# A one-core attention and FFN kernel: the hand-written orders of four engines are laid out anew

## Chip, cores and metric

The kernel runs on one core of a Trainium2 chip. The metric is the device time of one execution in microseconds (us), lower is better. The core has a matrix engine (TensorE, PE here, with its weight loads as PEld), VectorE (DVE), ScalarE (ACT), GpSimd (POOL) and a queue engine (SP) that issues transfers.

## What is computed

The reference, cut to what matters. The inputs x and ctx have shape (8, 128, 256): 8 batches, 128 channels that are 16 heads of 8, and 256 positions.

```
def xattn(k, v, q, taps, D):            # k = v = ctx, q = layernorm(x), 16 heads of 8
    kv = einsum('bhil,bhjl->bijhl', k, v)
    y = causal convolution of kv with taps[h] along l (length 256)
    out = y + kv * D[h]
    return einsum('bijhl,bhil->bjhl', out, q)
x = x + xattn(ctx, ctx, layernorm(x), taps, D)
h = layernorm(x)
x = x + (silu(h @ Wg.T) * (h @ Wu.T)) @ Wd.T     # W = (wq - 128) * s, 256 -> 704 -> 256
```

## The kernel before

The work runs in two stages that overlap. The first is the attention. For each of 16 heads `n` the products k_i k_j are made for 36 pairs of channels (`all_products` on DVE for heads 0 and 1; for the others `squares` on ACT and `pairs` on POOL). PE multiplies them with the head's Toeplitz matrix, which carries the taps and the skip D, in three float32 matmuls of 288 columns (`convolve_across`, `convolve_within`, together `convolve`; L985, L994, L996), two passes each. For heads 0 to 7 the matrix is loaded from memory, and DVE adds D to its diagonal (`direct`, L664). `multiply_terms(n)` on DVE (L731, L734, L738) multiplies the result, in PSUM, with q, in SBUF, and writes eight slots of terms. Two heads make a tile `t` of 128 rows of x, eight tiles in all.

q of a tile comes from a layernorm in small steps over three engines: `stats_of_q`, `moments_of_q`, `variance_of_q` on DVE, the power -1/2 `root_q` on POOL (L371), `shift_of_q` on DVE, `norm_q` on ACT (L488), a transposition by PE (`turn_q`, L939) and `evict_q` on ACT (L501, L504). The eight slots of a tile are summed by PE through transposing matmuls that accumulate in PSUM (`sum_terms`, L965). To spare PE, tiles 2 to 7 are merged beforehand: `merge_front` on POOL (L279), `merge_back` on DVE or, for tiles 5 to 7, on POOL (L287), and for tiles 3 to 7 `merge_last` on DVE (L296), which needs both others. ACT copies the wrapped channels first (`wrap`, L513), on which `merge_back` waits. Each merge reads two operands of 128x512 in SBUF and writes SBUF. `add_sum` on DVE adds the sum to x.

The second stage is the FFN, in four blocks `i` of two tiles. The same layernorm steps with the suffix f (`root_f`, L376), `turn_f` on PE (L947), then `high_f` on ACT and `low_f` on DVE (L717), which split the transposed rows in a high and a low float16 part. `gates(i, t)` on PE (L1018) gives gate and up for 128 hidden units (six chunks, the last one of 64), `gate` on ACT takes the silu, `hidden_units` on DVE (L746) the product, `hidden_high` on ACT and `low` on POOL or DVE (L257) split it in two parts. `downs` and `downs_last` on PE (L1037) multiply them with the third weight matrix, `scale_out` on DVE (L762) scales, `add` on POOL (L301) or `add_ffn` on DVE adds to x, and `store` sends the rows out. The convolutions use three PSUM tensors of two banks each (`conv`), which the gates share later; all transpositions of f, and of q from tile 6 on, and all sums share one bank (`turn`), so each must wait until its last reader is done.

Each engine executes its own list in order, and semaphores hold an instruction until what it needs is done. The lists are written out by hand, one call per line, at the end of each engine's function (POOL from L398, ACT from L545, DVE from L764, PE from L1060). Nothing else sets the order: a call that waits holds every call behind it on its engine. The waits stand in the helpers, for instance:

```
def sum_terms(t, free, count):
    ...
        wait(pe, all_merged, t + 1 - TWICE_MERGED)
    wait(pe, wrapped, t + 1)
...
def merge_last(eng, t):
    ...
    wait(eng, merged, t + 1 - UNMERGED)
    wait(eng, pool_back_merged if back_on_pool(t) else back_merged, back_count(t))
```

Of the kernel before, what the change touches and what calls it, by code (L numbers as in the profile page):

```python
# [74 lines left out]
def build(nc, x, ctx_skip, taps, matrices, wg_t, s_gate, wu_t, s_up, wd_t, s_down, taps_pad, out):  # L75
    with ExitStack() as ctx:
# [80 lines left out]
        q_ready = sem("q_ready")  # L157
# [210 lines left out]
        def _(pool):  # L368
# [77 lines left out]
            merge_front(nc.gpsimd, 5)  # L446
            pairs(15, 0, 2)
            merge_back(nc.gpsimd, 5)
            root_f(4)
            merge_front(nc.gpsimd, 6)  # L450
            low(0, 3)
            low(0, 4)
            merge_back(nc.gpsimd, 6)
            root_f(5)
            low(1, 0)
            low(1, 1)
            merge_front(nc.gpsimd, 7)
            low(1, 2)
            merge_back(nc.gpsimd, 7)
            root_f(6)  # L460
            add(0, 0)
            low(1, 3)
            low(1, 4)
            low(2, 0)
            root_f(7)
            low(2, 1)
            low(2, 2)
            add(0, 1)
            add(1, 0)
            add(1, 1)  # L470
            low(2, 3)
# [3 lines left out]
            low(3, 3)  # L475
            add(2, 0)
# [3 lines left out]
        def _(act):  # L480
# [75 lines left out]
            wrap(0)  # L556
            evict_q(1)
            act.wait_ge(k_loaded[3], 16)
            squares(4)
            norm_q(2)  # L560
            squares(5)
            squares(6)
            wrap(1)
            evict_q(2)
            squares(7)
            act.wait_ge(k_loaded[4], 16)
            squares(8)
            convert_gate()
            norm_q(3)
            wrap(2)  # L570
            squares(9)
            evict_q(3)
            norm_f(0)
            norm_q(4)
            convert_up()
            squares(10)
            high_f(0)
            evict_q(4)
            norm_f(1)
            squares(11)  # L580
            wrap(3)
            high_f(1)
            norm_q(5)
            convert_down()
            evict_q(5)
            act.wait_ge(scales_loaded, 3 * 16)
            gate(0, 0)
            wrap(4)
            gate(0, 1)
            hidden_high(0, 0)  # L590
            norm_q(6)
# [622 lines left out]
```

## Time and profile before

| | us |
|---|---|
| median of 3 runs | 76.41 |
| lowest, highest | 76.26, 76.46 |
| span of the profiled execution, first to last instruction | 74.5 |
| PE, DVE, POOL, ACT busy in it | 69.8, 61.7, 58.8, 45.5 |

No time of its own is given for the profiled execution beside its span; the median of the runs lies 1.9 us above that span. The profile gives for each engine its busy time, and for each instruction its start, its duration and what it waited for. Matmuls are pipelined: PE's rows overlap each other, and from one matmul to the next only the distance of their starts counts. The granted share of PE's clock was 0.997 over the span.

### The profile page before, as it was taken

The numbers are of one execution on the slowest core, as the hardware profiler recorded it, in microseconds if no ns is written. First come the engines' busy times: TensorE is split into PE (matmuls) and PEld (weight loads), VectorE is DVE, ScalarE is ACT, GpSimd is POOL, SyncE is SP. The second block draws the span as 40 slices with busy tenths as digits, with TensorE's granted clock in tenths as the row PEclk, the third lists the DMA queues.
The fourth block names the chain that finished last, engine by engine and source line by source line (L and its number), as shares of the span: only waits on it lengthen the run. The fifth ranks groups of instructions, "written<-read, shape, count | busy, mean of one in ns | idle before, by whom it ended". The sixth has DMA issues, their size and how long they took to land.

```text
span 74.5 us, 1494 instructions
## 1 busy us (share of the span) xinstructions
PE 69.8 (94%) x470; PEld 57.7 (77%) x470; DVE 61.7 (83%) x187; ACT 45.5 (61%) x115; POOL 58.8 (79%) x76
## 2 busy tenths in 40 slices
PE   5999989999999989999999999999999999999920
PEld 4666557988878848889798889797999989899810
DVE  0078899999988999999999899999968884586760
ACT  1503436464867879967746894657768796776400
POOL 6033587997999999899999999479998999339230
PEclk9999999999999999999999999999999999999998
DMA  0898999999997000000000000000002006000404
GB/s 8 235 254 230 372 315 364 324 382 392 361 356 224 29 0 0 0 0 4 9 0 0 0 0 4 0 0 0 0 13 70 0 0 210 1 9 0 140 1 141
DMA packets 7128, 8.29 MB, mean 111 GB/s; under 512 B 816, under 2 KB 6224, under 8 KB 7120
## 3 DMA queue, kind: packets, MB, share of 16 engines
q1 hardware_dynamic: 6768, 7.88, 33.0%
q10 hardware_dynamic: 352, 0.31, 1.2%
q8 instruction: 4, 0.07, 0.4%
q14 instruction: 4, 0.03, 0.2%
HBM read 7.12 MB, written 1.07 MB: 110 GB/s over the span
## 4 chain that ended last, share of the span: by engine, by line
PE 68%; POOL 16%; DVE 9%; issue 2%; ACT 1%; POOLq 0%; DVEq 0%
PE conv L1018 26%; PE down L1037 13%; POOL products L387 10%; PE conv L985 6%; PE turn L1058 5%; PE conv L994 5%; PE conv L996 5%; POOL rstd_q L371 4%; PE turn L965 3%; DVE terms L731 3%; PE turn L947 2%; PE turn L1037 2%; POOL terms L279 2%; DVE terms L734 1%; DVE terms L738 1%
## 5 line engine op out<-in xcount | busy, mean ns | idle before, releaser
L1018 PE MATMUL conv<-f_parts,wgu 128*128 128x256 f16 x176 | 22.1, 273 | 0.0
L387 POOL TENSOR_TENSOR products<-k_skip 128x512 f32<-128x512 f32 (+1 forms) x16 | 18.2, 1147 | 1.2 <-DMA k_skip<-ctx_skip 1.2
L1018 PEld LDWEIGHTS conv<-f_parts,wgu 128*128 128x128 f16 x176 | 16.6, 98 | 2.7 <-DVE hidden L746 0.2
L257 POOL TENSOR_TENSOR h_lo<-hidden,h_hi 128x256 fp32r<-128x256 f32 x18 | 13.1, 745 | 2.6 <-ACT h_hi L527 2.5
L746 DVE SCALAR_TENSOR_TENSOR hidden<-conv,su_sb,gate_act 128x256 f32<-128x256 f32 (+1 forms) x24 | 11.5, 482 | 3.0 <-ACT gate_act L522 2.8
L522 ACT ACTIVATE gate_act<-conv,sg_sb 128x256 f32<-128x256 f32 (+1 forms) x24 | 11.2, 467 | 4.2 <-PE conv L1018 3.9
L985 PE MATMUL conv<-products,toeplitz 128*128 128x288 f32 x32 | 11.3, 437 | 0.1
L731 DVE TENSOR_TENSOR terms<-conv,q_ext 128x512 f32<-128x512 f32 x16 | 10.9, 682 | 0.5 <-ACT q_ext L504 0.3
L994 PE MATMUL conv<-products,toeplitz 128*128 128x288 f32 x32 | 10.6, 413 | 0.3 <-DVE toeplitz L664 0.3
L996 PE MATMUL conv<-products,toeplitz 128*128 128x288 f32 x32 | 10.4, 406 | 0.0
L527 ACT ACTIVATE h_hi<-hidden 128x256 fp32r<-128x256 f32 x20 | 8.3, 413 | 3.4 <-DVE hidden L746 3.1
L1037 PE MATMUL down<-wd,h_hi 128*128 128x256 f32 x35 | 9.8, 307 | 0.0
L1037 PE MATMUL down<-wd,h_lo 128*128 128x256 f32 x35 | 8.8, 280 | 0.0
L734 DVE TENSOR_TENSOR terms<-conv,q_ext 128x384 f32<-128x384 f32 x16 | 8.8, 549 | 0.0
L488 ACT ACTIVATE q_rows<-x_sb,shift_q,rstd_q 128x256 f32<-128x256 f32 x8 | 4.8, 595 | 6.2 <-DVE shift_q L689 6.2
L279 POOL TENSOR_TENSOR terms<-terms 128x512 f32<-128x512 f32 x6 | 8.4, 1396 | 0.0
L965 PE MATMUL turn<-ident,terms 128*128 128x128 f32 x60 | 7.9, 273 | 0.0
L994 PEld LDWEIGHTS conv<-products,toeplitz 128*128 128x128 f32 x32 | 6.1, 197 | 2.3 <-issue 1.0
L965 PEld LDWEIGHTS turn<-ident,terms 128*128 128x128 f32 x60 | 7.0, 141 | 0.9
L996 PEld LDWEIGHTS conv<-products,toeplitz 128*128 128x128 f32 x32 | 6.1, 190 | 1.7
L371 POOL TENSOR_TENSOR rstd_q<-variance_q,minus_half 128x1 f32<-128x1 f32 x8 | 5.3, 664 | 2.6 <-DVE variance_q L684 2.6
L1037 PEld LDWEIGHTS down<-wd,h_hi 128*128 128x128 f32 x35 | 6.6, 189 | 0.5 <-DVE h_lo L257 0.2
(64 smaller groups left out, 121.6 us busy)
## 6 DMA issues: line engine op xcount, KB each, us to landing
k_skip<-ctx_skip SPq DMA_DIRECT2D x3, 384.0 KB, 5.9
toeplitz<-taps_pad SPq DMA_DIRECT2D x2, 512.0 KB, 8.6
out<-x_sb SPq DMA_DIRECT2D x7, 128.0 KB, 1.7
toeplitz<-matrices SPq DMA_DIRECT2D x3, 256.0 KB, 5.4
wg_int<-wg_t SPq DMA_DIRECT2D x1, 704.0 KB, 7.6
wu_int<-wu_t SPq DMA_DIRECT2D x1, 704.0 KB, 8.8
wd_int<-wd_t SPq DMA_DIRECT2D x1, 640.0 KB, 10.0
x_sb<-x SPq DMA_DIRECT2D x1, 512.0 KB, 5.1
```

Source lines behind the costliest of these rows:

```text
L257: eng.tensor_tensor(low_of(i, t), hidden[up_lanes(t), i % 2, t, :], high_of(i, t), ALU.subtract).then_inc(done, 1)
L279: eng.tensor_tensor(even, even, odd, ALU.add).then_inc(merged, 1)
L387: nc.gpsimd.tensor_tensor(view(products[:, n:n + 1], first * MADE + GROUP, [[MADE, halves], [GROUP, 4], [1, GROUP]]), view(k, 0, [[EXT * B ...
L522: nc.scalar.activation(gate_act[up_lanes(t), i % 2, t, :], gate_of(i, t), ACT.Silu, scale=sg_sb[gate_lanes(t), t:t + 1]).then_inc(gate_act ...
L731: dve.tensor_tensor(view(z, h, [[TERMS, HALVES], [P, 4], [to, GROUP]]), view(y, HALF0, [[COLS, HALVES], [GROUP, 4], [1, GROUP]]), view(q, ...
L746: dve.scalar_tensor_tensor(out=hidden[lanes, i % 2, t, :], in0=up_of(i, t), scalar=su_sb[lanes, t:t + 1], in1=gate_act[lanes, i % 2, t, :] ...
L965: done = nc.tensor.matmul(turned[:, c * P:(c + 1) * P], view(z, c * TERMS + slot, [[1, P]]), ident[:, :], is_transpose=True, start=(n == 0 ...
L985: nc.tensor.matmul(conv[BUFFER[n]][:, BANK:BANK + COLS], toeplitz[:, n, P:L], products[:, n, 0:COLS], start=True, stop=False)
L994: nc.tensor.matmul(y[:, BANK:BANK + COLS], within, products[:, n, MADE:MADE + COLS], start=False, stop=True)
L996: nc.tensor.matmul(y[:, HALF0:BANK], within, products[:, n, 0:COLS], start=True, stop=True).then_inc(conv_done, 1)
L1018: done = nc.tensor.matmul(bank_of(i, t)[:, n, :], wgu[:, c, column:column + P], f_parts[:, i % 2, part, c, :], start=(c == 0 and part == 0 ...
L1037: done = nc.tensor.matmul(down_of(i, r), part[:, r * P:(r + 1) * P], wd[:, t, :], start=own, stop=(t == FULL), skip_group_check=True)
```

## The change

The same calls stand in the four lists, in another order. No call, instruction or transfer is added or removed, and each stays on its engine; the helpers, their waits and SP's list are untouched. On POOL the roots are gathered in groups; on DVE the first variance comes ahead of the products, `merge_back(3)`, `merge_back(4)` and `merge_last(3)` stand together, and most statistics and multiplies shift by a few places; on ACT the squares of heads 9 to 14 come earlier, and the highs and gates are regrouped; on PE `turn_q(0)` stands ahead of `convolve_within(0)`, and some turns, sums, gates and downs change places. The diff is long; this is its part on POOL around the heads 4 to 14:

```diff
-            root_q(2)
             pool.wait_ge(k_loaded[3], 16)
             pairs(4, 0, 2)
+            root_q(2)
+            root_q(3)
             pairs(5, 0, 2)
             pairs(6, 0, 2)
-            root_q(3)
             pairs(7, 0, 2)
-            root_f(0)
             pool.wait_ge(k_loaded[4], 16)
             pairs(8, 0, 2)
+            pairs(9, 0, 2)
             merge_front(nc.gpsimd, 2)
             root_q(4)
-            pairs(9, 0, 2)
+            root_q(5)
+            root_f(0)
             root_f(1)
+            root_q(6)
             pairs(10, 0, 2)
-            root_q(5)
             pairs(11, 0, 2)
+            merge_front(nc.gpsimd, 3)
             pool.wait_ge(k_loaded[5], 16)
             pairs(12, 0, 2)
-            root_q(6)
-            merge_front(nc.gpsimd, 3)
-            root_q(7)
+            pairs(13, 0, 2)
+            pairs(14, 0, 2)
             merge_front(nc.gpsimd, 4)
             low(0, 0)
             root_f(2)
-            pairs(13, 0, 2)
-            root_f(3)
             low(0, 1)
             low(0, 2)
-            pairs(14, 0, 2)
```

and this its part on DVE around the merges of tiles 3 and 4:

```diff
             multiply_terms(8)
+            moments_of_q(7)
             low_f(1)
+            shift_of_q(6)
+            variance_of_q(7)
+            multiply_terms(9)
+            stats_of_f(2)
             merge_back(dve, 3)
-            multiply_terms(9)
-            variance_of_q(7)
+            merge_back(dve, 4)
             merge_last(dve, 3)
-            merge_back(dve, 4)
             dve.wait_ge(scales_loaded, 3 * 16)
             hidden_units(0, 0)
-            shift_of_q(6)
             hidden_units(0, 1)
+            add_sum(3)
+            multiply_terms(10)
             moments_of_f(2)
-            add_sum(3)
+            stats_of_f(3)
             variance_of_f(2)
-            stats_of_f(3)
```

Three places of the program as it is built. POOL's list from `pairs(10)` to `low(0, 0)` before (`products` are the pairs, `rstd` the roots, `terms` the merges of two halves of the slots, `h_lo` a low part):

```order
L387 TENSOR_TENSOR products<-k_skip 128x2x256
L371 TENSOR_TENSOR rstd_q<-variance_q,minus_half 128x1
L387 TENSOR_TENSOR products<-k_skip 128x2x256 x2
L371 TENSOR_TENSOR rstd_q<-variance_q,minus_half 128x1
L279 TENSOR_TENSOR terms<-terms 128x2x2x128
L371 TENSOR_TENSOR rstd_q<-variance_q,minus_half 128x1
L279 TENSOR_TENSOR terms<-terms 128x2x2x128
L257 TENSOR_TENSOR h_lo<-hidden,h_hi 128x256
```

and in the change, from `merge_front(2)` to `low(0, 0)`:

```order
L279 TENSOR_TENSOR terms<-terms 128x2x2x128
L371 TENSOR_TENSOR rstd_q<-variance_q,minus_half 128x1 x2
L376 TENSOR_TENSOR rstd_f<-variance_f,minus_half 128x1 x2
L371 TENSOR_TENSOR rstd_q<-variance_q,minus_half 128x1
L387 TENSOR_TENSOR products<-k_skip 128x2x256 x2
L279 TENSOR_TENSOR terms<-terms 128x2x2x128
L387 TENSOR_TENSOR products<-k_skip 128x2x256 x3
L279 TENSOR_TENSOR terms<-terms 128x2x2x128
L257 TENSOR_TENSOR h_lo<-hidden,h_hi 128x256
```

Five roots now stand in one group, and from the pairs of head 10 on there is no root between the pairs and merges up to the low part. DVE's list from `low_f(1)` (L717) over `multiply_terms(9)` (L731 to L738) to the first `hidden_units` before, with `merge_last` as L296 and `merge_back` as L287:

```order
L717 TENSOR_TENSOR f_parts<-turn,f_parts 128x2x128
L287 TENSOR_TENSOR terms<-terms 128x2x2x128
L731 TENSOR_TENSOR terms<-conv,q_ext 128x2x256
L734 TENSOR_TENSOR terms<-conv,q_ext 128x2x3x64
L738 TENSOR_TENSOR terms<-conv,q_ext 128x2x64
L684 TENSOR_SCALAR variance_q<-moments_q 128x1
L296 TENSOR_TENSOR terms<-terms 128x2x2x128
L287 TENSOR_TENSOR terms<-terms 128x2x2x128
L746 SCALAR_TENSOR_TENSOR hidden<-conv,su_sb,gate_act 128x256
```

and in the change:

```order
L731 TENSOR_TENSOR terms<-conv,q_ext 128x2x256
L734 TENSOR_TENSOR terms<-conv,q_ext 128x2x3x64
L738 TENSOR_TENSOR terms<-conv,q_ext 128x2x64
L699 BN_STATS stats_f<-x_sb 128x6
L287 TENSOR_TENSOR terms<-terms 128x2x2x128 x2
L296 TENSOR_TENSOR terms<-terms 128x2x2x128
L746 SCALAR_TENSOR_TENSOR hidden<-conv,su_sb,gate_act 128x256 x2
```

The three merges that stood around the multiply and a variance now follow each other. Third, the beginning of DVE's list before:

```order
L676 BN_STATS stats_q<-x_sb 128x6
L670 TENSOR_TENSOR products<-k_skip 128x320
L680 BN_AGGR moments_q<-stats_q 128x2
L670 TENSOR_TENSOR products<-k_skip 128x320
L664 SCALAR_TENSOR_TENSOR toeplitz<-anti,k_skip,toeplitz 128x128
L684 TENSOR_SCALAR variance_q<-moments_q 128x1
L689 TENSOR_SCALAR shift_q<-moments_q,rstd_q 128x1
L670 TENSOR_TENSOR products<-k_skip 128x320 x2
```

and in the change:

```order
L676 BN_STATS stats_q<-x_sb 128x6
L680 BN_AGGR moments_q<-stats_q 128x2
L684 TENSOR_SCALAR variance_q<-moments_q 128x1
L670 TENSOR_TENSOR products<-k_skip 128x320
L664 SCALAR_TENSOR_TENSOR toeplitz<-anti,k_skip,toeplitz 128x128
L689 TENSOR_SCALAR shift_q<-moments_q,rstd_q 128x1
L670 TENSOR_TENSOR products<-k_skip 128x320 x3
```

The variance of tile 0 moved ahead of all products, and a product moved behind the shift.

## Rows read from the trace of the kernel before

**Rows 1.** The page: the span, and part 1, busy us (share) xinstructions.

```profile
span 74.5 us, 1494 instructions
...
PE 69.8 (94%) x470; PEld 57.7 (77%) x470; DVE 61.7 (83%) x187; ACT 45.5 (61%) x115; POOL 58.8 (79%) x76
```

**Rows 2.** Who waited for whom: total us, times, longest us.

```profile
PE turn L947 <- DVE f_parts L717: 0.3, 1, 0.3
```

**Rows 3.** The chain that ended last: start us, us, what.

```profile
20.29 1.23 POOL terms L279
...
27.15 0.41 PE turn L947 x2
```

**Rows 4.** Timeline of DVE, start: start us, us, instruction, idle before.

```profile
5.05 0.15 DVE L684 TENSOR_SCALAR variance_q<-moments_q 128x1 f32<-128x1 f32 x1
...
8.04 0.69 DVE L731 TENSOR_TENSOR terms<-conv,q_ext 128x512 f32<-128x512 f32 x1 [0.26 <-ACT q_ext L504]
```

**Rows 5.** Timeline of ACT, start.

```profile
6.20 0.60 ACT L488 ACTIVATE q_rows<-x_sb,shift_q,rstd_q 128x256 f32<-128x256 f32 x1 [3.25 <-DVE shift_q L689]
```

**Rows 6.** Timeline of PE.

```profile
6.94 0.41 PE L939 MATMUL down<-ident,q_rows 128*128 128x128 f32 x2
...
9.86 0.72 PE L994 MATMUL conv<-products,toeplitz 128*128 128x288 f32 x2 [0.26 <-DVE toeplitz L664]
...
23.29 0.65 PE L985 MATMUL conv<-products,toeplitz 128*128 128x288 f32 x2
...
26.16 0.65 PE L996 MATMUL conv<-products,toeplitz 128*128 128x288 f32 x2
...
32.34 0.60 PE L965 MATMUL turn<-ident,terms 128*128 128x128 f32 x4
```

**Rows 7.** Timeline of SP's queue.

```profile
8.76 0.34 SPq L323 DMA_DIRECT2D k_skip<-ctx_skip  x1
```

**Rows 8.** Timeline of POOL.

```profile
12.42 3.88 POOL L387 TENSOR_TENSOR products<-k_skip 128x512 f32<-128x512 f32 x3
...
21.49 1.04 POOL L371 TENSOR_TENSOR rstd_q<-variance_q,minus_half 128x1 f32<-128x1 f32 x1
...
23.75 0.54 POOL L376 TENSOR_TENSOR rstd_f<-variance_f,minus_half 128x1 f32<-128x1 f32 x1
...
28.47 0.56 POOL L371 TENSOR_TENSOR rstd_q<-variance_q,minus_half 128x1 f32<-128x1 f32 x1
28.99 1.53 POOL L279 TENSOR_TENSOR terms<-terms 128x512 f32<-128x512 f32 x1
30.78 0.93 POOL L371 TENSOR_TENSOR rstd_q<-variance_q,minus_half 128x1 f32<-128x1 f32 x1 [0.26 <-DVE variance_q L684]
...
43.17 1.65 POOL L279 TENSOR_TENSOR terms<-terms 128x512 f32<-128x512 f32 x1
```

**Rows 9.** Timeline of DVE, its merges.

```profile
21.46 0.66 DVE L287 TENSOR_TENSOR terms<-terms 128x512 f32<-128x512 f32 x1
...
28.69 0.68 DVE L287 TENSOR_TENSOR terms<-terms 128x512 f32<-128x512 f32 x1
...
30.61 0.68 DVE L296 TENSOR_TENSOR terms<-terms 128x512 f32<-128x512 f32 x1
31.22 0.69 DVE L287 TENSOR_TENSOR terms<-terms 128x512 f32<-128x512 f32 x1
...
43.00 0.68 DVE L296 TENSOR_TENSOR terms<-terms 128x512 f32<-128x512 f32 x1
...
47.54 0.69 DVE L296 TENSOR_TENSOR terms<-terms 128x512 f32<-128x512 f32 x1
```

**Rows 10.** Groups by line and shape: busy us, mean ns, idle before.

```profile
L301 POOL TENSOR_TENSOR x_sb<-x_sb,ffn_out 128x256 f32<-128x256 f32 x7 | 5.2, 756 | 1.8 <-DVE ffn_out L762 1.8
```

**Rows 11.** Busy time by stretch: us, busy (x) by engine, granted clock, DMA.

```profile
core 0: us, PE busy (x) PEld busy (x) DVE busy (x) ACT busy (x) POOL busy (x), PEclk, DMA share, GB/s
...
40.00:50.00 10.00, 10.00 (x71) 8.47 (x70) 9.63 (x28) 6.85 (x18) 8.48 (x10) 1.00 0.00 1
```

More of the change, by code:

```diff
@@ L475, in _ @@
             low(3, 3)
+            add(1, 1)
             add(2, 0)
@@ L787, in _ @@
             direct(3)
+            shift_of_q(1)
             dve.wait_ge(x_loaded[2], 16)
             stats_of_q(2)
-            shift_of_q(1)
+            stats_of_q(3)
+            multiply_terms(1)
             moments_of_q(2)
-            multiply_terms(1)
+            moments_of_q(3)
             variance_of_q(2)
-            stats_of_q(3)
+            variance_of_q(3)
             dve.wait_ge(direct_loaded[3], 16)
@@ L809, in _ @@
-            direct(6)
+            stats_of_q(5)
+            add_sum(1)
             moments_of_f(0)
-            shift_of_q(3)
-            multiply_terms(4)
+            moments_of_q(5)
+            stats_of_f(1)
+            merge_back(dve, 2)
+            variance_of_q(4)
+            variance_of_q(5)
             variance_of_f(0)
+            moments_of_f(1)
+            stats_of_q(6)
             direct(7)
-            variance_of_q(4)
-            multiply_terms(5)
-            add_sum(1)
@@ L818, in _ @@
-            shift_of_f(0)
-            stats_of_q(5)
-            stats_of_f(1)
-            stats_of_q(6)
-            moments_of_q(5)
-            moments_of_f(1)
-            merge_back(dve, 2)
-            shift_of_q(4)
-            moments_of_q(6)
-            variance_of_f(1)
+            moments_of_q(6)
+            shift_of_q(4)
+            stats_of_q(7)
+            variance_of_f(1)
+            shift_of_q(5)
+            add_sum(2)
+            variance_of_q(6)
+            shift_of_f(0)
@@ L854, in _ @@
[L854 removed]
+            hidden_units(0, 2)
             moments_of_f(3)
+            merge_last(dve, 4)
             shift_of_f(2)
[L857 to L859 removed]
             multiply_terms(11)
             add_sum(4)
+            variance_of_f(3)
             hidden_units(0, 3)
[L863 removed]
+            hidden_units(0, 4)
             shift_of_f(3)
[L865 removed]
+            shift_of_q(7)
@@ L868, in _ @@
             low_f(3)
+            hidden_units(0, 5)
+            stats_of_f(4)
+            merge_last(dve, 5)
+            multiply_terms(13)
             moments_of_f(4)
-            shift_of_q(7)
+            hidden_units(1, 0)
+            low(0, 5)
             variance_of_f(4)
-            multiply_terms(13)
-            merge_last(dve, 5)
+            multiply_terms(14)
+            add_sum(5)
             shift_of_f(4)
-            hidden_units(0, 5)
-            hidden_units(1, 0)
-            add_sum(5)
-            multiply_terms(14)
             stats_of_f(5)
@@ L924, in _ @@
             scale_out(2, 1)
+            low(3, 1)
             hidden_units(3, 4)
@@ L1097, in _ @@
             gates(0, 2)
+            gates(0, 3)
             turn_q(6, x1_ready, 4)
-            gates(0, 3)
-            downs(0, 0)
             convolve(12)
@@ L1103, in _ @@
             gates(0, 4)
+            downs(0, 0)
             turn_f(2, x1_ready, 5)
```

192 lines of the change are left out of this document (90 added, 102 removed).

## The prediction

> **What bounds the kernel now.** The page comes first: TensorE (PE) holds an instruction for 69.8 of 74.5 us, VectorE (DVE) for 61.7, POOL for 58.8 [rows 1]. One core runs; the profiled execution spans 74.5 us, 1.9 us less than the 76.41 us median of the runs, and I carry those 1.9 us unchanged, so every difference below is added to 76.41. The list of who waited for whom shows what is left on PE: from 10 us on there is one wait, of 0.3 us, in front of a turn (L947) [rows 2]. The chain of waits says the same: from that turn at 27.15 us on it stays on PE to the last matmul. Before, it runs through POOL and DVE, as in the sum on POOL (L279) of 20.29 us [rows 3]. So the kernel is PE bound from 27 us on, with DVE and POOL close behind. Only about 3 us of PE's time are not steady work, and a new order can gain no more than that. It can lose without such a limit: each engine works its list in order, so one late instruction holds all behind it.
>
> **The start.** `variance_of_q(0)` moves ahead of DVE's products. It began at 5.05 us with two products (L670) and one `direct` (L664) ahead of it [rows 4]; now it begins at about 4.25. The root on POOL still has to pass the add to the taps that ends at 4.45, so `norm_q(0)`, which began at 6.20 us [rows 5], begins at about 5.35, and `turn_q(0)`, now in front of `convolve_within(0)`, at 6.1 instead of 6.94 [rows 6]. PE itself wins nothing there: the first convolution ends at 7.3 us instead of 7.2. But q is ready 0.8 us sooner, so `multiply_terms(0)` begins with its convolution, 7.5 instead of 8.04 [rows 4]. Its 1.3 us are then over at 8.8, when the matrices of heads 2 and 3 land (SP, which waits for the same transfer, goes on at 8.76 [rows 7]). `convolve_across(2)` starts at 8.88 as before, bound by that landing, but `direct(2)` no longer stands behind the multiply, and `convolve_within(2)` starts at 9.4 instead of 9.86 [rows 6]. Gain 0.4 us. With one root on POOL less in front of `pairs(4)` it grows to about 0.6 at 14.3 us.
>
> **18 to 31 us.** POOL's roots are gathered: q2 and q3 together, and q4, q5, f0, f1 and q6 after `merge_front(2)`. The pairs, 1.24 us from start to start in a run of three [rows 8], therefore come up earlier, `merge_front(2)` at 19.3 instead of 20.3 [rows 3]. `direct(7)` now stands behind `merge_back(2)`, the variances and `stats_of_q(6)`, and `convolve_within(7)` needs it. Following DVE's steps from rows of the same kind, `direct(7)` ends at 21.7 to 22.2, PE waits 0.1 to 0.9 us, and the 0.6 us are given back in the worse case (PE reaches `convolve(8)` at 22.8 or 23.3, before at 23.29 [rows 6]). Then a true gain: before, `turn_f(1)` waited for `low_f(0)` and began at 27.15, although the last matmuls of the convolution ahead of it began at 26.16 and take 0.49 us from start to start: 0.5 us lost [rows 2, 6]. Now `low_f(0)` ends 0.5 to 1.0 us sooner, and PE is the later one. So `convolve(11)` ends at 31.7 (31.3 at best) instead of 32.34 [rows 6]. So far the gain is 0.6 us (1.0 at best).
>
> **The three merges, on which the forecast rests.** `sum_terms(3)` needs `merge_last(3)`. Before, DVE did `merge_back(3)`, `multiply_terms(9)`, `merge_last(3)`, `merge_back(4)` at 28.69, 30.61 and 31.22 us [rows 9], and on POOL at those moments stood a root (28.47 and 30.78), never a long instruction [rows 8]. Now the three merges stand in one piece, and POOL, which has had its roots already, is inside `pairs(12)`, `pairs(13)`, `pairs(14)`, `merge_front(4)`, four instructions in a row of 1.25 us or more. What do a merge on DVE and one on POOL do to each other? Both read two operands in SBUF. The rows show one direction. The root at 21.49 us took 1.04 us against 0.54 for the one at 23.75 [rows 8], and beside it DVE had the merge of 21.46 us (0.66) [rows 9]: it finished as if it had begun at that merge's end. The sum at 28.99 took 1.53 instead of the 1.23 of 20.29 us [rows 3], and that of 43.17 took 1.65, both begun beside a DVE merge (28.69, 43.00) [rows 8, 9]. DVE's multiplies of one operand in PSUM and one in SBUF do no such thing: three pairs from 12.42 us on took 3.88 us beside two of them, 1.29 each. So POOL waits for the rest of a DVE instruction with two SBUF operands. The other direction the trace does not show: none of the eight merges and eight `direct`s on DVE starts in the middle of a long POOL instruction. Its price lies between 0 (DVE passes) and the whole rest of POOL's instruction, up to 1.25 us for each merge. I take the upper end, because what POOL shows is a full stop and not a slowing, which fits one holder at a time better than a preference. And who comes next when both wait? The root of 30.78 us waited for `merge_last(3)`, and ended at 31.71, half a microsecond after that merge, although `merge_back(4)` was next in DVE's queue at 31.22 [rows 8, 9]: the engine that waits gets its turn in between, and no block of merges is kept whole. (`merge_back(4)` lost nothing, as a root reads one column.)
>
> By that: on DVE `low_f(0)` ends at 26.4, two multiplies of 1.27 us with `low_f(1)` (0.34) and small steps between them end at 29.55, `stats_of_f(2)` at 29.9, and `merge_back(3)` is ready. On POOL `root_q(6)` ends at 24.0, two pairs at 26.5, `merge_front(3)` at 27.7, and `pairs(13)` runs from 28.95 to 30.2, so the merge falls into its middle. It runs 30.2 to 30.8; `pairs(14)` 30.8 to 32.05; `merge_back(4)` to 32.65; `merge_front(4)` to 33.9; `merge_last(3)` to 34.6. `sum_terms(3)` starts at 34.75 instead of 32.34: PE stands still for 3.0 us, less the 0.6 us won before, is **2.4 us lost**. Nothing later on PE can win it back, as PE was full.
>
> The Trainium skill, "SBUF — State Buffer", section "SBUF: two separate sides", says this outright: the port pair that VectorE and GpSimd share is an exclusive lock, taken by whichever starts first for its whole instruction, also by a VectorE instruction with two SBUF inputs against a GpSimd one that reads SBUF. By that rule the sum is the 2.4 us above, and without it the first rival below; the trace agrees for POOL (1.04 against 0.54 us) and no run here shows it for DVE.
>
> **After that.** `merge_last(5)`, `low(0, 5)` and `merge_last(6)` may meet `low(0, 3)`, `merge_front(6)` and `low(0, 4)` on POOL: 0 to 1.2 us together. DVE has little room at 43 to 50 us (9.63 of 10 us busy at 40 to 50 [rows 11]). Against it, small waits of PE between 33 and 62 us, 0.1 us here and there, can go: 0 to 0.4. I take 0 for the sum of both. The moved `downs` and `gates` swap places on a full PE and cost nothing. At the end `add(1, 1)` stands behind `low(3, 3)`, 0.7 us of POOL [rows 10], with 1.8 us of waiting in front of POOL's last add before [rows 10], so it stays covered, and its store too. Sum: 76.4 + 2.4 = **78.8 us**, in this case 78.0 to 79.7 (one merge more or less lucky, and 1.2 us of later meetings).
>
> **Rivals.**
> 1. *POOL's long instructions do not stop DVE.* Then the merges run 29.4 to 31.3, `sum_terms(3)` starts at 31.45, 0.9 us sooner than before, and the waits of PE that go later add 0 to 0.4 us, while new ones of 0.1 us where DVE is full take as much back: 75.5 us (75.1 to 75.9). For it: no DVE row is ever lengthened, roots of POOL beside merges cost the merges nothing (0.68 beside them, 0.69 alone [rows 9]). Against it: POOL's full stops. Chance 0.25.
> 2. *DVE is stopped once, but then keeps its turn through all three.* `merge_last(3)` ends at 32.15 and `sum_terms(3)` starts at 32.3, as before; later 0.5 us either way: 76.4 (75.9 to 76.9). The root of 31.71 us speaks against it. Chance 0.15.
> 3. The forecast, the engines taking turns: chance 0.60. It comes out slower; the rival with the other sign is the first. It decides at one point: if `merge_back(4)` and `merge_last(3)` each begin within 0.1 us of the merge ahead, the forecast has fallen.
>
> **The numbers.** A measurement of this kernel tells about 0.3%, 0.23 us. Rival 1 gives 0.24 faster and 0.01 same, rival 2 0.04, 0.06 and 0.05, the forecast 0.60 slower less 0.02 same: faster 0.28, same 0.09, slower 0.63. The range for all cases runs from rival 1's middle to the upper part of the forecast, 75.4 to 79.5; the likeliest case's own range is 78.0 to 79.7.
>
> **What would show it.** Right: a wait of PE of 2 to 3 us in front of the L965 matmuls of `sum_terms(3)`, ended by DVE's L296; between DVE's L287 and L296 rows gaps, or rows of 1.3 to 1.9 us, each as long as a POOL instruction beside it; `turn_f(1)` without a wait; `norm_q(0)` at 5.3 us. Wrong: three merges 0.61 us from start to start while POOL's pairs are lengthened instead. A wait of 3 us could also let the granted clock of PE fall, which stood at 1.00 in the stretch of 40 to 50 us [rows 11]; I sum nothing for it. That PE's instructions are the same in number and kind leaves only waits to change its time.

## The result, and the profile of the changed kernel

| us | before | changed |
|---|---|---|
| median | 76.40 | 81.75 |
| lowest, highest | 76.26, 76.46 | 80.62, 84.06 |
| span of the profiled execution | 74.5 | 78.7 |
| its own time | 76.4 by the 1.9 us carried | 80.62 |
| PE, DVE, POOL, ACT busy in it | 69.8, 61.7, 58.8, 45.5 | 70.2, 67.8, 59.7, 46.3 |

The changed kernel is slower: the ratio is 1.058, with an interval of 1.0548 to 1.0609, or about 80.8 us. I had predicted 78.8 us and a range of 75.4 to 79.5, so the sign was right and the time lies above the range. The median stands above the ratio because two of the four executions, 82.60 and 84.06 us, showed a lower mean granted clock (0.970 and 0.977) and are left out of the ratio. The profiled one is the 80.62 us one, and its span is 4.2 us longer than before's.

The page, span and part 1:

```profile
span 78.7 us, 1494 instructions
...
PE 70.2 (89%) x470; PEld 57.4 (73%) x470; DVE 67.8 (86%) x187; ACT 46.3 (59%) x115; POOL 59.7 (76%) x76
```

Against [rows 1] PE is as busy as it was and stands still for longer, and DVE is busy for 6.1 us more with the same 187 instructions. So DVE instructions became longer. PE's timeline shows where PE first pays:

```profile
6.26 0.41 PE L939 MATMUL down<-ident,q_rows 128*128 128x128 f32 x2 [0.46 <-ACT q_rows L488]
...
9.44 0.72 PE L994 MATMUL conv<-products,toeplitz 128*128 128x288 f32 x2
...
21.70 1.06 PE L965 MATMUL turn<-ident,terms 128*128 128x128 f32 x8 [0.17 <-issue]
...
23.63 0.65 PE L985 MATMUL conv<-products,toeplitz 128*128 128x288 f32 x2
...
26.98 0.38 PE L947 MATMUL turn<-ident,f_rows 128*128 128x128 f32 x2
...
31.59 0.65 PE L996 MATMUL conv<-products,toeplitz 128*128 128x288 f32 x2
34.54 0.66 PE L965 MATMUL turn<-ident,terms 128*128 128x128 f32 x4 [2.30 <-DVE terms L296]
...
50.68 0.44 PE L947 MATMUL turn<-ident,f_rows 128*128 128x128 f32 x2 [0.66 <-ACT f_rows L493]
```

`sum_terms(3)` (L965) starts at 34.54 us against 32.34 in [rows 6], after a wait that `merge_last(3)` ends. The reason stands on DVE. Its timeline, the merges, the low parts (L257) and the adds to the diagonal (L664):

```profile
8.95 1.07 DVE L664 SCALAR_TENSOR_TENSOR toeplitz<-anti,k_skip,toeplitz 128x128 f32<-128x128 f32 x2
...
20.56 1.04 DVE L287 TENSOR_TENSOR terms<-terms 128x512 f32<-128x512 f32 x1
...
30.08 1.07 DVE L287 TENSOR_TENSOR terms<-terms 128x512 f32<-128x512 f32 x1
31.06 1.75 DVE L287 TENSOR_TENSOR terms<-terms 128x512 f32<-128x512 f32 x1
32.74 1.75 DVE L296 TENSOR_TENSOR terms<-terms 128x512 f32<-128x512 f32 x1
...
44.19 0.90 DVE L296 TENSOR_TENSOR terms<-terms 128x512 f32<-128x512 f32 x1
46.96 1.14 DVE L257 TENSOR_TENSOR h_tail<-hidden,h_tail 64x256 fp32r<-64x256 f32 x1
51.15 0.91 DVE L296 TENSOR_TENSOR terms<-terms 128x512 f32<-128x512 f32 x1
...
57.49 1.07 DVE L296 TENSOR_TENSOR terms<-terms 128x512 f32<-128x512 f32 x1
...
71.07 0.96 DVE L257 TENSOR_TENSOR h_lo<-hidden,h_hi 128x256 fp32r<-128x256 f32 x1
72.98 0.62 DVE L257 TENSOR_TENSOR h_lo<-hidden,h_hi 128x256 fp32r<-128x256 f32 x1
73.63 0.84 DVE L257 TENSOR_TENSOR h_tail<-hidden,h_tail 64x256 fp32r<-64x256 f32 x1
```

and POOL's:

```profile
9.02 2.84 POOL L387 TENSOR_TENSOR products<-k_skip 128x256 f32<-128x256 f32 x3
...
19.79 1.26 POOL L279 TENSOR_TENSOR terms<-terms 128x512 f32<-128x512 f32 x1
...
29.33 1.26 POOL L387 TENSOR_TENSOR products<-k_skip 128x512 f32<-128x512 f32 x1
30.56 1.71 POOL L387 TENSOR_TENSOR products<-k_skip 128x512 f32<-128x512 f32 x1
32.23 1.71 POOL L279 TENSOR_TENSOR terms<-terms 128x512 f32<-128x512 f32 x1
...
46.55 1.27 POOL L279 TENSOR_TENSOR terms<-terms 128x512 f32<-128x512 f32 x1 [0.33 <-DVE terms L738]
...
57.27 1.88 POOL L257 TENSOR_TENSOR h_lo<-hidden,h_hi 128x256 fp32r<-128x256 f32 x2
...
71.02 0.73 POOL L257 TENSOR_TENSOR h_lo<-hidden,h_hi 128x256 fp32r<-128x256 f32 x1 [0.57 <-ACT h_hi L527]
71.71 2.48 POOL L301 TENSOR_TENSOR x_sb<-x_sb,ffn_out 128x256 f32<-128x256 f32 x3
```

Read the two together from 29.33 us on. The merge of 30.08 is over at 31.15, which is 0.56 us after the end of `pairs(13)` (30.59). `pairs(14)`, begun at 30.56, is 1.71 long instead of 1.26: it waited for that merge and ends at 32.27. `merge_back(4)`, begun at 31.06, is over at 32.81, `merge_front(4)`, begun at 32.23, at 33.94, and `merge_last(3)` at 34.49. Each instruction ends one work time after the one on the other engine: 0.54 to 0.56 us for a DVE merge, 1.12 or 1.13 for a long POOL one. They take turns, as the forecast's case had it. The three merges took 4.4 us from first start to last end, where three lone ones would take 1.9.

How far each call on PE starts behind its start before tells where the 4.2 us come from: 0.34 us behind at `convolve(8)`, 0.26 us ahead at `convolve(11)` with the old wait of `turn_f(1)` gone, then behind by 2.20 at `sum_terms(3)`, 3.02 at `gates(1, 3)`, 3.26 at `gates(3, 0)`, 3.6 at `downs_last(3, 0)` and 4.2 at the last.

### The profile page after: what moved, and what is told of

It is laid out like the page before. It is cut to its first block, busy times and chain, and to the rows that moved or that the text cites. A ratio compares the mean times of both kernels' runs of the same rounds, so it can differ in the third digit from the quotient of the medians.

```text
span 78.7 us, 1494 instructions
## 1 busy us (share of the span) xinstructions
PE 70.2 (89%) x470; PEld 57.4 (73%) x470; DVE 67.8 (86%) x187; ACT 46.3 (59%) x115; POOL 59.7 (76%) x76
## 3 DMA queue, kind: packets, MB, share of 16 engines
HBM read 7.12 MB, written 1.07 MB: 104 GB/s over the span
## 4 chain that ended last, share of the span: by engine, by line
PE 56%; DVE 21%; ACT 11%; issue 4%; DMA 4%; POOL 1%; DVEq 0%; POOLq 0%
PE conv L1018 16%; PE down L1037 9%; PE turn L965 9%; PE conv L994 6%; PE conv L996 6%; PE conv L985 5%; DMA x_sb<-x 4%; DVE terms L296 3%; PE turn L947 3%; DVE h_tail L257 3%; DVE terms L731 3%; DVE hidden L746 2%; ACT q_rows L488 2%; ACT gate_act L522 2%; PE down L939 2%
## 5 line engine op out<-in xcount | busy, mean ns | idle before, releaser
L1018 PE MATMUL conv<-f_parts,wgu 128*128 128x256 f16 x176 | 21.4, 273 | 0.0
L387 POOL TENSOR_TENSOR products<-k_skip 128x512 f32<-128x512 f32 (+1 forms) x16 | 18.9, 1205 | 1.9 <-DMA k_skip<-ctx_skip 1.9
L257 POOL TENSOR_TENSOR h_lo<-hidden,h_hi 128x256 fp32r<-128x256 f32 x18 | 13.6, 775 | 4.0 <-ACT h_hi L527 4.0
L731 DVE TENSOR_TENSOR terms<-conv,q_ext 128x512 f32<-128x512 f32 x16 | 10.9, 682 | 0.0
L527 ACT ACTIVATE h_hi<-hidden 128x256 fp32r<-128x256 f32 x20 | 7.7, 413 | 5.2 <-DVE hidden L746 5.1
L985 PE MATMUL conv<-products,toeplitz 128*128 128x288 f32 x32 | 10.6, 418 | 0.1
L994 PE MATMUL conv<-products,toeplitz 128*128 128x288 f32 x32 | 10.5, 410 | 0.0
L996 PE MATMUL conv<-products,toeplitz 128*128 128x288 f32 x32 | 10.4, 406 | 0.0
L965 PE MATMUL turn<-ident,terms 128*128 128x128 f32 x60 | 8.0, 275 | 2.5 <-DVE terms L296 2.3
L965 PEld LDWEIGHTS turn<-ident,terms 128*128 128x128 f32 x60 | 6.7, 141 | 4.3 <-DVE terms L296 3.1
L376 POOL TENSOR_TENSOR rstd_f<-variance_f,minus_half 128x1 f32<-128x1 f32 x8 | 4.8, 604 | 4.2 <-DVE variance_f L707 4.2
```

Source lines behind the costliest of these rows:

```text
L257: eng.tensor_tensor(low_of(i, t), hidden[up_lanes(t), i % 2, t, :], high_of(i, t), ALU.subtract).then_inc(done, 1)
L387: nc.gpsimd.tensor_tensor(view(products[:, n:n + 1], first * MADE + GROUP, [[MADE, halves], [GROUP, 4], [1, GROUP]]), view(k, 0, [[EXT * B ...
L731: dve.tensor_tensor(view(z, h, [[TERMS, HALVES], [P, 4], [to, GROUP]]), view(y, HALF0, [[COLS, HALVES], [GROUP, 4], [1, GROUP]]), view(q, ...
L965: done = nc.tensor.matmul(turned[:, c * P:(c + 1) * P], view(z, c * TERMS + slot, [[1, P]]), ident[:, :], is_transpose=True, start=(n == 0 ...
L985: nc.tensor.matmul(conv[BUFFER[n]][:, BANK:BANK + COLS], toeplitz[:, n, P:L], products[:, n, 0:COLS], start=True, stop=False)
L994: nc.tensor.matmul(y[:, BANK:BANK + COLS], within, products[:, n, MADE:MADE + COLS], start=False, stop=True)
```

## The experiments

Each says from which kernel its edit starts. Ratios are to before. Lengths and starts are those of one traced execution of each kernel. At `convolve(8)` the traces of kernels with the whole start of the change differ by up to 1 us (from 0.19 us ahead of before in write_only to 0.77 behind in pairs_later), so small differences between two traces are taken from one common call to the next.

### Is it the overlap? keep_off, pairs_later

keep_off, from the changed kernel, holds POOL back until the merges are done:

```diff
             pairs(12, 0, 2)
+            pool.wait_ge(all_merged, 1)
             pairs(13, 0, 2)
```

> The changed kernel with one wait more: POOL begins pairs(13), pairs(14) and merge_front(4) only when merge_last(3) on DVE is done. All orders stay. If POOL's long instructions stop DVE's merges in turn (the forecast's theory), the three merges now take 0.61 us from start to start, merge_last(3) ends at about 32.0 instead of 34.48 us, PE's wait in front of sum_terms(3) is under 0.2 us instead of 2.3, and the time falls by 1.5 to 2.3 us against the change (80.9 to 78.6-79.4), less what POOL's two lost microseconds cost later. If the merges were late for another reason (their semaphores, DVE's own load), they stay 1.0 to 1.75 us long, and the time stays or grows.

Measured: 79.94 us (79.08 to 80.12), ratio 1.0424 [1.0365, 1.0484]. DVE's timeline, and POOL's:

```profile
30.39 1.28 DVE L287 TENSOR_TENSOR terms<-terms 128x512 f32<-128x512 f32 x2
31.58 0.68 DVE L296 TENSOR_TENSOR terms<-terms 128x512 f32<-128x512 f32 x1
...
36.21 1.20 DVE L296 TENSOR_TENSOR terms<-terms 128x512 f32<-128x512 f32 x1 [0.57 <-POOL terms L279]
```

```profile
32.41 2.53 POOL L387 TENSOR_TENSOR products<-k_skip 128x512 f32<-128x512 f32 x2 [2.74 <-DVE terms L296]
34.89 1.28 POOL L279 TENSOR_TENSOR terms<-terms 128x512 f32<-128x512 f32 x1
```

With POOL empty the merges are 0.68 us each again, and `sum_terms(3)` starts at 32.38 without a wait, 2.16 us sooner. That shows that the overlap alone made the wait. But `merge_front(4)` on POOL now begins 2.7 us later and ends at 36.17, `merge_last(4)` waits for it and is 1.20 long itself, and PE waits 1.15 us ahead of `sum_terms(4)` and 0.58 ahead of `turn_f(2)`. Most of the gain comes back as those, and the time is above the 78.6 to 79.4 us expected.

pairs_later, from the changed kernel, takes two of the long instructions out of the stretch instead:

```diff
-            pairs(13, 0, 2)
-            pairs(14, 0, 2)
             merge_front(nc.gpsimd, 4)
             low(0, 0)
             root_f(2)
+            pairs(13, 0, 2)
+            pairs(14, 0, 2)
```

> The changed kernel with pairs(13) and pairs(14) behind root_f(2) on POOL, near where they stood before. By the turn-taking theory merge_back(3) meets merge_front(4) alone (about 1.1 us long), merge_back(4) and merge_last(3) are 0.68, merge_last(3) ends at about 33.0 us, PE waits 0.8 us instead of 2.3: 1.0 to 1.5 us less than the change. If a block of merges was merely late for its semaphores, no change (within 0.3 us).

Measured: 81.53 us (81.48 to 81.72), 1.0660 [1.0614, 1.0705]. The expected gain was missed. One long instruction is left, and one merge is stopped, `merge_back(3)`, 1.65 us beside `merge_front(4)`; the other two are 0.68. The three merges take 1.56 us less than in the changed kernel and begin 0.43 us later, like the whole start in this execution, and `sum_terms(3)` starts at 33.41, 1.1 us sooner. But the two pairs and the roots behind them are now late, and from `turn_f(3)` on PE is 1.0 to 1.1 us behind the changed kernel, 0.4 of it from the start.

### The triple in the order of before: triple_before

From before:

```diff
-            merge_back(dve, 3)
             multiply_terms(9)
             variance_of_q(7)
+            merge_back(dve, 3)
+            merge_back(dve, 4)
             merge_last(dve, 3)
-            merge_back(dve, 4)
```

> The kernel before, with one piece of the change alone: merge_back(3), merge_back(4) and merge_last(3) stand together on DVE, behind multiply_terms(9) and variance_of_q(7). POOL keeps its order of before, with a root in front of each merge_front. By the turn-taking theory merge_back(3) runs beside root_q(7) or is held by merge_front(3) for under 0.3 us, then merge_front(4) comes in between: merge_back(4) 1.2 to 1.8 us long, merge_last(3) free, sum_terms(3) at 33.2 to 33.8 instead of 32.34 us and the time 0.9 to 1.4 us over the kernel before. If DVE's merges pass POOL's sums, under 0.2 us.

Measured: 77.7 us (77.61 to 78.35), 1.0174 [1.0111, 1.0237], within what was expected. DVE's timeline, then POOL's:

```profile
29.95 0.82 DVE L287 TENSOR_TENSOR terms<-terms 128x512 f32<-128x512 f32 x1
31.11 0.69 DVE L287 TENSOR_TENSOR terms<-terms 128x512 f32<-128x512 f32 x1 [0.34 <-ACT terms L513]
31.72 1.75 DVE L296 TENSOR_TENSOR terms<-terms 128x512 f32<-128x512 f32 x1
```

```profile
30.17 1.01 POOL L371 TENSOR_TENSOR rstd_q<-variance_q,minus_half 128x1 f32<-128x1 f32 x1
31.15 1.77 POOL L279 TENSOR_TENSOR terms<-terms 128x512 f32<-128x512 f32 x1
```

With three merges together, but roots on POOL in part of the stretch, one merge meets a long POOL instruction and is stopped for 1.07 us; `sum_terms(3)` starts 1.19 us late and the kernel is 1.3 us slower. `merge_last(3)` begins 1.11 us later than before, and before it was over 1.05 us ahead of `sum_terms(3)`, so without its stop next to nothing would have been lost. I had named `merge_back(4)` as the stopped one; it was `merge_last(3)`.

### Which POOL instructions stop DVE: write_only, read_one

Both from keep_off, whose POOL is empty beside the merges. write_only puts two fills of 1024 elements a row there, read_one two scalings that read one operand of 512 in SBUF and write SBUF; what they write is overwritten later.

```diff
+            nc.gpsimd.memset(ffn_out[:, :, :, :], 0.0)
+            nc.gpsimd.memset(hidden[:, 1, 0:4, :], 0.0)
             pool.wait_ge(all_merged, 1)
```

```diff
+            nc.gpsimd.tensor_scalar(ffn_out[:, 0, :, :], x_sb[:, 6:8, :], 1.5, None, ALU.mult)
+            nc.gpsimd.tensor_scalar(ffn_out[:, 1, :, :], x_sb[:, 6:8, :], 1.5, None, ALU.mult)
             pool.wait_ge(all_merged, 1)
```

> keep_off with two more POOL instructions beside the three merges, which only write: memsets of 1024 elements into the place of ffn_out and of block 1 of hidden, both overwritten later. If any POOL instruction stops DVE's merges, one or two of them are 1.0 us or longer; if only one that reads SBUF does, all three are 0.68, and so are the memsets unlengthened.

> keep_off with two more POOL instructions beside the three merges, which read one operand of 512 elements in SBUF (x) and write one (the place of ffn_out). If one read operand is enough to stop DVE, merges beside them are over 0.9 us; if it takes two, all are 0.68.

Measured in one execution each: 79.13 and 81.21 us. DVE's and POOL's timelines of write_only:

```profile
29.55 1.27 DVE L287 TENSOR_TENSOR terms<-terms 128x512 f32<-128x512 f32 x2
30.74 0.68 DVE L296 TENSOR_TENSOR terms<-terms 128x512 f32<-128x512 f32 x1
```

```profile
28.75 0.97 POOL L437 MEMSET ffn_out<- 128x1024 f32 x1
29.64 0.97 POOL L438 MEMSET hidden<- 128x1024 f32 x1
```

and of read_one:

```profile
30.38 1.27 DVE L287 TENSOR_TENSOR terms<-terms 128x512 f32<-128x512 f32 x2
31.58 0.68 DVE L296 TENSOR_TENSOR terms<-terms 128x512 f32<-128x512 f32 x1
```

```profile
29.62 1.49 POOL L437 TENSOR_SCALAR ffn_out<-x_sb 128x512 f32<-128x512 f32 x1
31.08 2.53 POOL L438 TENSOR_SCALAR ffn_out<-x_sb 128x512 f32<-128x512 f32 x1
```

A fill neither stops nor is stopped: the first is mostly alone and the second beside two merges, both take 0.97 us, and the merges keep 0.68. A scaling with one operand does not stop the merges either, though one begins in its middle (30.38), but the second scaling is 1.04 us longer than the first, as if it had stood until the last merge was over. So in these runs DVE was stopped only where both instructions read two operands in SBUF. That one read operand never stops DVE is not shown: the scaling is the only such instruction tried beside a merge, in one execution, and it is also another operation.

### The later meetings: low_later, add_back, tail_back

low_later, from the changed kernel, moves the low part of 46.96 us away from `merge_front(6)`:

```diff
             hidden_units(1, 0)
-            low(0, 5)
...
             merge_last(dve, 6)
+            low(0, 5)
             low_f(4)
```

> The changed kernel with low(0, 5) behind merge_last(6) on DVE, where it stood before. In the change it lasted 1.14 us beside merge_front(6) and PE then waited 0.7 us for norm_f(4) in front of turn_f(4). If that stop is the cause, multiply_terms(14) and all behind it come 1.1 us sooner, PE's wait there goes and the time falls by 0.5 to 0.8 us. If another wait stands right behind it (merge_last(6), root_f(4)), by under 0.3 us.

Measured: 81.36 us (80.58 to 82.01), 1.0565 [1.048, 1.0651]: no gain. The wait of 0.82 us ahead of `turn_f(4)` is gone, and the one ahead of `sum_terms(6)` grew from 0.32 to 0.95 us, since `low(0, 5)` and `merge_last(6)` now meet `low(0, 4)` and `low(1, 0)`, 0.84 and 0.89 us long. This execution also shows the clock. PE stood until 34.50 as in the changed kernel, and then the busy time by stretch reads (columns as in [rows 11]):

```profile
35.00:36.00 1.00, 1.00 (x10) 0.82 (x8) 1.00 (x3) 1.00 (x3) 0.64 (x1) 0.76 0.00 0
36.00:37.00 1.00, 1.00 (x6) 0.73 (x5) 1.00 (x5) 0.65 (x2) 0.09 (x1) 0.50 0.00 0
37.00:38.00 1.00, 1.00 (x7) 0.78 (x5) 1.00 (x5) 0.00 (x0) 0.59 (x2) 0.50 0.00 0
38.00:39.00 1.00, 1.00 (x5) 0.86 (x4) 1.00 (x3) 0.86 (x3) 0.97 (x1) 0.53 0.00 0
39.00:40.00 1.00, 1.00 (x6) 0.77 (x5) 0.77 (x3) 0.90 (x3) 0.50 (x1) 1.00 0.03 8
```

and in the changed kernel's own execution

```profile
35.00:40.00 5.00, 5.00 (x39) 4.23 (x38) 5.00 (x16) 3.42 (x9) 3.28 (x5) 1.00 0.02 5
```

In low_later the granted clock is 0.50, the lower of its two levels (1.2 GHz), from 35.5 to 38.9 us, after PE had waited 2.3 us and worked for 1.0. The sixteen matmuls of two `gates` take 3.11 us there instead of 1.91, and at `sum_terms(4)` PE is 1.5 us behind the changed kernel. The fastest execution, 80.58 us at a mean granted clock of 1.000, is level with the changed kernel's 80.62, so the mend gained nothing at the full clock either.

add_back, from the changed kernel, returns the add of the end to its old place; tail_back adds the old order of ACT's and DVE's last gates, highs and lows to it:

```diff
             add(1, 0)
+            add(1, 1)
             low(2, 4)
...
             low(3, 3)
-            add(1, 1)
```

```diff
             gate(3, 0)
+            hidden_high(3, 0)
             gate(3, 1)
             gate(3, 2)
-            hidden_high(3, 0)
             hidden_high(3, 1)
-            hidden_high(3, 2)
             gate(3, 3)
+            hidden_high(3, 2)
...
+            low(3, 1)
             hidden_units(3, 3)
             scale_out(2, 0)
             scale_out(2, 1)
-            low(3, 1)
```

> The changed kernel with POOL's add(1, 1) back in front of low(2, 4), so that it stands no more among the last low parts. By the theory that POOL's adds stop DVE's low(3, 1), low(3, 4) and low(3, 5) (0.96, 0.62 and 0.84 us against 0.42), these fall to 0.42 to 0.6 us and the time falls by 0.4 to 0.9 us. If the end is late only because PE's work came late, the time stays within 0.2 us.

> The changed kernel with the last block's order of before: add(1, 1) ahead of low(2, 4) on POOL, low(3, 1) ahead of hidden_units(3, 3) on DVE, one hidden_high between the gates of block 3 on ACT. If the late adds and highs cost the end its last microsecond (scale_out(2) late, so that add(2, 0) and add(2, 1) fall on low(3, 4) and low(3, 5)), the lows are 0.42 us each and the time is 0.7 to 1.0 us under the change. If not, within 0.3 us of it.

Measured: add_back 81.11 us (80.41 to 81.8), 1.0515 [1.045, 1.058]; tail_back 81.09 (79.92 to 81.85), 1.0479 [1.0394, 1.0563]. The intervals overlap each other's and that of the changed kernel, so only the traces tell. In add_back `low(3, 5)` is 0.42 us instead of 0.84, and PE gains 0.41 us between `downs_last(4, 0)` and `downs_last(5, 0)`; the other two low parts stay long (0.96 and 0.63), against what I expected. In tail_back `low(3, 5)` is 0.42 and `low(3, 1)` 0.62, but `low(3, 4)` is 0.82, longer than the 0.62 of the changed kernel. The last matmul comes 0.63 us sooner, of which 0.14 was there at `gates(3, 0)`, ahead of every edit; the fastest execution is 0.7 us faster (79.92 against 80.62). The old end gives back 0.5 us of the 0.9 that PE lost behind `gates(3, 0)`.

### All mends together: three_mends

It is keep_off with the edits of tail_back and low_later.

> The changed kernel with the wait of keep_off and the edits of tail_back and low_later together. If these three stops are what the change lost, the time is near the kernel before or under it: 76.4 to 78.0 us. If each mend only uncovers the next wait, it stays over 78.5.

Measured: 79.09 us (79.03 to 79.11), 1.0337 [1.0288, 1.0385]. The mends do not add up. PE waits 1.15 us ahead of `sum_terms(4)`, 0.58 ahead of `turn_f(2)`, 0.94 ahead of `sum_terms(6)`, and 0.67 at the end. What the new order lost is not three places that can be set right one by one. The gain of one is the wait of the next.

### The start alone: start_only, start_wait, start_turn

start_only, from before, takes the change's start: its first variance, product and shift on DVE, `variance_of_q(1)` ahead of `multiply_terms(0)`, `turn_q(0)` ahead of `convolve_within(0)`.

```diff
             stats_of_q(0)
+            moments_of_q(0)
+            variance_of_q(0)
             dve.wait_ge(k_loaded[0], 16)
             all_products(0, 0, 1)
-            moments_of_q(0)
-            all_products(0, 1, 2)
...
             direct(0)
-            variance_of_q(0)
             shift_of_q(0)
+            all_products(0, 1, 2)
...
-            convolve_within(0)
             pe.wait_ge(ident_ready, 1)
             turn_q(0, q_ready, 0)
+            convolve_within(0)
```

> The kernel before with the change's start alone: moments and variance of tile 0 ahead of the products, turn_q(0) ahead of convolve_within(0), the second product behind the shift, variance_of_q(1) ahead of multiply_terms(0). By the prediction's own steps convolve_within(2) starts at 9.4 instead of 9.86 us; if the 0.4 us carry through to 27 us the time falls by 0.3 to 0.5 us (76.4 to 76.0), if the chain over POOL and DVE up to turn_f(1) has its own pace, by under 0.2 us.

Measured: 76.59 us (75.75 to 76.92, 12 executions), 1.0000 [0.9965, 1.0035]. Three executions lie at 75.75 to 75.77, the others at 76.41 and above, so the expected gain shows in three of twelve. The trace is of one at 75.75: there `direct(2)` and `direct(3)` run from 8.81 to 9.41 and the pairs of head 3 on POOL begin at 9.15, behind the start of `direct(3)`, and PE is 0.56 to 0.59 us ahead to the end. In the changed kernel the same pairs begin at 9.02, and the two `direct` take 1.07 us. So I fixed who comes first:

```diff
             root_q(1)
+            pool.wait_ge(direct_ready, 4)
             pairs(3, 0, 1)
```

> start_only with one wait more: POOL begins pairs(3) only when direct(3) is done. start_only had two groups of times, 75.75 and 76.4 to 76.9 us. If the second group is the executions in which pairs(3) on POOL started ahead of direct(2) or direct(3) and stopped it, all times now lie at 75.7 to 75.9 us, 0.5 to 0.6 us under the kernel before. If the groups come from the landing of the transfers alone, they stay.

Measured: 75.82 us (75.73 to 76.32), ratio 0.9954 [0.9932, 0.9976]. This is 0.5% under the kernel before, clear of the noise, and under the changed kernel. In the trace the two `direct` take 0.60 us, and POOL's pairs of head 3 begin at 9.50, and 0.78 us of waiting on POOL cost nothing. But I had expected all times at 75.7 to 75.9, and three of the eight executions are at 76.16, 76.21 and 76.32. The other traces show a second meeting in the same start. In keep_off the pairs of head 2, released by their transfer, begin just ahead of `direct(1)` (DVE, then POOL):

```profile
6.49 0.82 DVE L665 SCALAR_TENSOR_TENSOR toeplitz<-anti,k_skip,toeplitz 128x128 f32<-128x128 f32 x1
```

```profile
6.42 1.47 POOL L387 TENSOR_TENSOR products<-k_skip 128x256 f32<-128x256 f32 x2 [1.30 <-DMA k_skip<-ctx_skip]
```

Where these pairs begin behind `direct(1)`, as at 7.13 us in the changed kernel, `direct(1)` takes 0.35 us. It is stopped like this (0.81 to 0.82) in the traces of keep_off, pairs_later, read_one and three_mends, and at `sum_terms(0)` PE is there 0.3 to 0.4 us behind the changed kernel. The wait in start_wait holds back only the pairs of head 3, so this stop would fit its three slower executions; it is not shown, as none of them was traced.

In start_wait's trace `turn_f(1)` still waits 0.53 us for `low_f(0)`. start_turn goes for that:

```diff
             add_sum(2)
-            stats_of_q(7)
             shift_of_f(1)
-            moments_of_q(7)
             variance_of_q(5)
-            stats_of_f(2)
             multiply_terms(7)
             low_f(0)
             shift_of_q(5)
             variance_of_q(6)
+            stats_of_q(7)
+            moments_of_q(7)
+            stats_of_f(2)
             multiply_terms(8)
```

> start_wait with three small statistics on DVE (stats_of_q(7), moments_of_q(7), stats_of_f(2)) set behind low_f(0) and shift_of_q(5), variance_of_q(6), instead of ahead of multiply_terms(7). low_f(0), which began at 26.02 us there and held turn_f(1) back by 0.53 us, should begin at about 25.2. My theory of the early part: DVE's lateness at low_f(0) is all that holds turn_f(1), and merge_last(3), over at 30.7 us, covers a sum_terms(3) that then starts at 31.25 instead of 31.77 us. So turn_f(1) starts at 26.05 without a wait, every later call on PE comes 0.4 to 0.5 us sooner, and the time is 75.3 to 75.5 us. Rival: behind it DVE or POOL is as full as PE, and the 0.5 us come back as small waits from 30 us on: then 75.7 to 76.0 us.

Measured: 76.14 us (75.83 to 76.36), 0.9971 [0.9947, 0.9995]. No gain over start_wait. PE's timeline:

```profile
26.16 0.38 PE L948 MATMUL turn<-ident,f_rows 128*128 128x128 f32 x2
...
28.55 1.91 PE L1019 MATMUL conv<-f_parts,wgu 128*128 128x256 f16 x16 [0.33 <-DVE f_parts L718]
```

The wait ahead of `turn_f(1)` is gone and stands ahead of `gates(0, 0)`, which needs `low_f(1)`: 0.50 us, and 0.17 more ahead of `convolve(11)`. DVE had as much work as before ahead of `low_f(1)`, only in another order. The rival that I had given for it was right in kind, a full DVE; its time (75.7 to 76.0) was still too low, and the waits came at 28.6 us already and not from 30 us on.

## Why the prediction was right and wrong

- **The triple, the step on which it rested: right.** `sum_terms(3)` was to start at 34.75 and did at 34.54. The merges were to end at 30.8, 32.65 and 34.6, and did at 31.15, 32.81 and 34.49, in turn with POOL as written. Rival 1 (POOL doesn't stop DVE) falls by the rows of 1.07 and 1.75 us, rival 2 (DVE keeps its turn) by the second one of 1.75. keep_off shows the cause by taking POOL away. The loss of 2.2 us against my 2.4 is closer than its parts: PE stood for 2.5 us instead of 3.0, and had won 0.26 us before instead of 0.6, and the two misses partly cancel, which is luck.
- **The start: right up to 9 us, then a stop that I left out.** `norm_q(0)` was to begin at 5.35 and did at 5.52, `turn_q(0)` at 6.1 and did at 6.26, `convolve_within(2)` at 9.4 and did at 9.44. But the products of head 3 now meet `direct(3)`, which has two SBUF operands like a merge. It was the same mechanism as in my main step, and I did not go through the start with it. In the changed kernel `turn_q(1)` waits 0.4 us behind it, and start_wait, where it is kept out, is the faster kernel. The meeting of `direct(1)` with the pairs of head 2 was left out as well.
- **"So far the gain is 0.6 us (1.0 at best)": wrong.** It was 0.26 us at the end of `convolve(11)`. `merge_back(2)` was met by `merge_front(2)` and took 1.04 instead of 0.66, so `sum_terms(2)` waited 0.33 us at 21.70, and `convolve(8)` started at 23.63, beyond the worse of my two values (23.3). `direct(7)`, to which I had given the wait, cost PE nothing. `turn_f(1)` without a wait was right, and of its 0.5 us 0.3 only paid that back. How much hangs on the start alone shows in write_only, whose lists are those of the changed kernel up to 28 us: `direct(1)` and `direct(3)` are not stopped there, `convolve(8)` starts at 23.10, within my two values, and `sum_terms(3)`, with no long POOL instruction beside the triple, at 31.55, 0.79 us ahead of before, although `merge_back(2)` is stopped there too (1.02 us). In keep_off, where `direct(1)` and `direct(3)` are stopped, it starts at 32.38.
- **"I take 0 for the sum of both": the step that failed most, a term put at nothing.** I had given the later meetings 0 to 1.2 us, set gains of 0 to 0.4 against them, and took nothing for both. They cost 1.1 us: the delay grows from 2.20 us at `sum_terms(3)` to 3.26 at `gates(3, 0)`, by `turn_f(4)` (0.82 us of waiting), `sum_terms(6)` (0.32) and `gates(2, 2)` (0.21), 1.35 us together, of which other small waits that went gave back 0.3. So both terms stood in my text with fitting sizes, and what had no reason was to let them cancel. DVE's room, 9.63 of 10 us busy [rows 11], was what should have told that a longer DVE instruction goes straight to PE there. low_later shows that the first of the three waits came from `low(0, 5)`, as it went when that call was moved. The other two are read from the rows: just ahead of the last one `merge_last(7)`, which I had not listed, takes 1.07 us beside POOL's low parts of 57.27.
- **"It stays covered": wrong.** I costed `add(1, 1)` by POOL's own waiting. What it does is to meet DVE: with it and the adds behind it in one run of three, the low parts of 71.07, 72.98 and 73.63 us met POOL instructions, and PE lost 0.9 us behind `gates(3, 0)`, where I had put nothing. add_back, which moves this add alone, took 0.4 of them back, and tail_back 0.5. The rest is not taken apart by a run.
- **"I sum nothing for it": half right.** In the profiled execution the clock stayed at 1.00 after the wait; in that of low_later it fell and took about 1.5 us. That the changed kernel's executions of 82.60 and 84.06 us have this cause is not shown, as no trace of them was taken; the slower of the two has the higher mean clock (0.977 against 0.970), so the clock can't be all of it.
- **One reading of a row.** The 1.23 us with which I compared the sum of 28.99 is the chain's share of that instruction [rows 3]; its own length in the timeline is 1.27. That leaves 0.26 us of delay instead of 0.30 and doesn't change the argument.

By the sum: 76.4, plus 2.2 instead of 2.4 at `sum_terms(3)`, plus 1.1 instead of 0, plus 0.9 instead of 0, is 80.6, the profiled execution's time. With the upper 1.2 us that I had named for the meetings, the forecast would have been 80.0, short by 0.6: the end's 0.9, less the 0.2 too much at the merges and the 0.1 too much for the meetings. And the top of my range, 79.5, lay under these 80.0, so it left out what my own terms allowed.

The Trainium skill, "SBUF — State Buffer", section "SBUF: two separate sides", states the main step. The traces agree where both engines read two operands (1.75 against 0.68 us), and where the GpSimd instruction reads nothing (0.97 us fills, merges 0.68). By the section a GpSimd instruction that reads SBUF should also have stopped the merge that started in its middle in read_one; it took 0.67 there, and the measurement decides.

## What to carry to other kernels

Before DVE and POOL lists are reordered, write down every pair of instructions on the two that would overlap and of which both read two SBUF operands, over the whole kernel, its start included, and not only at the one place that looks worst. Each stop here cost DVE up to 1.1 us beside an instruction of 1.26, and where DVE had no room most of it went to the end time. A block of such DVE instructions should stand beside POOL's short ones (roots of one column, as the merges did before, or fills). And where a single place is mended, ask which call has next to no slack behind it: in keep_off, pairs_later, low_later, three_mends and start_turn the wait moved elsewhere.

## What the runs showed of the hardware that was not expected

- In one execution a POOL scaling with one SBUF operand did not stop a DVE merge (0.67 us) but a second one was itself held, 2.53 against 1.49 us; it got no turn between two merges, while POOL instructions of two operands did.
- DVE multiplies with one operand in PSUM (L731) were never stopped: the sixteen of the changed kernel take 0.67 to 0.69 us each, whatever POOL does.
- The same wait of 2.3 us on PE was followed by a granted clock of 0.50 for about 3.4 us in one execution (low_later) and of 1.00 in three others (the changed kernel, add_back, tail_back).
- One program had two groups of times (start_only, 75.75 us, and 76.4 us and more). With a wait on POOL that fixes who comes first at 9 us, five of eight executions lie at 75.73 to 75.84 and three at 76.16 to 76.32; none is at 76.4 or more. That two meetings make the slower times, of `direct(3)` with the pairs of head 3 and of `direct(1)` with those of head 2, fits this, but no execution of the slower groups was traced.
